# A Mamba block and a feed-forward block on one core: the group scale-and-shift, the end statistics, two bank places and one convolution tap change their place

## The chip, the cores and the metric

The kernel runs on one core of a Trainium2 chip. The metric is device time in microseconds (us), from the launch's first to its last instruction, the median of three runs. The engines of the core are TensorE (PE, matrix products; PEld is its weight load), VectorE (DVE), ScalarE (ACT), GpSimd (POOL) and SyncE (SP, which here only starts DMAs). Each has its own stream of instructions, runs it in the order in which it was written, and waits for the others on semaphores.

## The reference, cut to what matters

```python
# x is (8, 1024, 256) in float32: 8 batches, 1024 tokens, 256 channels
x = x + layernorm(attn(layernorm(x)))      # attn is a Mamba block
x = x + layernorm(ffn(layernorm(x)))       # ffn has weights of one sign bit and a scale

def attn(x):                               # 512 inner channels, 8 heads of 64
    xi, z = x @ Wx.T, x @ Wz.T
    xi = silu(causal_conv(xi, 4 taps) + conv_b)
    B, C = xi @ Wb.T, xi @ Wc.T
    dt = softplus(xi @ Wdt.T + b_dt)
    y = ssd_scan(xi, B, C, dt, -exp(log_a)) + d_param * xi
    y = (y - mean) / sqrt(var + eps) * gn_w + gn_b     # over all tokens and the 64 channels of a head
    return (y * silu(z)) @ Wout.T

def ffn(x):                                # 256 -> 1024 -> 256
    return gelu(x @ bw1.T + b1) @ bw2.T + b2
```

The group norm needs the whole sequence of a batch before its first output. So all that follows it (gate, output product, both residual sums, the feed-forward block) is a **tail** of the batch that can only begin when the batch's scan is through.

## The kernel before, in words

**Tiling.** A batch has 1024 tokens in two blocks j of 512 (BLK), and each block has four chunks q of 128 tokens. Channels lie on partitions, c counts the four groups of 128 inner channels (KI). `yT` holds the scan's output of a whole batch, `zs` the silu of the gate.

**Turns.** `turn_steps` writes one list of steps, a turn. In turn b the steps marked `own` belong to batch b, those marked `tail` to batch b-1, and a few at the end (`next`) to batch b+1. All five engines walk the same list (`all_batches`, `run`), and each carries out those steps for which it has a handler. So the list sets the order on each engine and nothing else does. There are eight turns; turn 0 has no tail steps, and after turn 7 comes `last_tail`. Turns 1 to 6 are alike.

**The steps that matter here**, with the lines of the profile:

- `xi` is the product with Wx (PE L1497) and two reads of its bank by ACT: the copy (L946) and the last tap with the bias (L953). `conv` is the other three taps on DVE (L1137); for (j, c) = (0, 0) they run in place in `hh`, lent for that time. Its two last arguments say which of the three taps are made. `silu` (ACT L981) and `xs_hi` (ACT L988) follow, `xs` (DVE L1142) makes the low half.
- `gn_sum` (DVE L1280 to L1285), `gn_mean` (PE L1652), `gn_root` (DVE L1289 to L1295, POOL L776) and `gn_fold` (DVE L1300 to L1304) turn the statistics of a batch into a scale and a shift for each channel. I call the application of the two to `yT` the **fold**: in the kernel before it is ACT's handler of the step `gate` (`head_normalise`, L1056), four instructions of 256 tokens for each (j, m). The other handlers of `gate` multiply by `zs`: DVE for j = 0 (L1311), POOL for j = 1 (L802). `Wo` is the output product (PE L1667 for j = 0), whose half m waits for the four gates of that half.
- `mid_stat`, `mid_norm`, `ff_stat`, `ff_norm` are the two layer norms around the residual sum. `ff_norm` writes `un` on ACT (L905). It waits for the root on POOL, which waits for the statistics on DVE. `uT` turns `un` on PE (L1507) and splits it on ACT (L1072) and DVE (L1339) into `uh`; `H` is the first feed-forward product (PE L1682), `O` the second (L1695).
- For each chunk: `ends` and `front` (PE L1598, L1579, L1587; `xdt` on DVE L1241; `Cd` and `xdw` on POOL L825 and L818), `score` (PE L1609, then `mt` on DVE L1250), `carry` (PE L1623 and L1632, the running `state` on POOL L836 and DVE L1256) and `back` (PE L1645, then `yT` on DVE L1266). The product L1623 of a chunk waits for its `xdw`, and the next chunk's L1632 for the new `state`.
- `end_stat` is the statistics of the last layer norm, on DVE (L1097 to L1107). It waits for POOL's bias sum (L788), the last part of `O`. `end_root` is on POOL (L766, L770), `end_norm` on ACT (L905, writes `y`), `end_add` on POOL (L793).

**Banks.** PSUM has eight banks. Five are the ring of the `own` steps: their products take the banks in turn, in the order of the list, and a product waits until the bank's last product has been read. A `None` in the list of keys skips one place, so that from there on the pairs (product, product before it in the same bank) are other ones. Two banks are the tail's, one is for the turned input and its like.

Of the kernel before, what the change touches and what calls it, by code (L numbers as in the profile page):

```python
# [20 lines left out]
NJ = T // BLK  # L21
NQ = BLK // P
# [116 lines left out]
def turn_steps(first, last):  # L139
# [16 lines left out]
    steps = []  # L156
    for j in range(NJ):
# [10 lines left out]
        elif j == 0:  # L168

            steps += own(("silu", 0, 0), ("xs_hi", 0, 0), ("xi", 0, 1), ("xi", 0, 2), ("xi", 0, 3))  # L170
            steps += tail(("head_stat", NJ - 1, 1), ("gn_sum",), ("gn_mean",)) + own(("conv", 0, 1, 0, 1)) + tail(("gn_root",))
            steps += own(("conv", 0, 1, 1, 3), ("z", 0, 0)) + tail(("gn_fold",)) + own(("conv", 0, 2, 0, 1), ("z", 0, 1))
            steps += tail(("gate", 0, 0)) + own(("xs", 0, 0), ("silu", 0, 1), ("xs_hi", 0, 1), ("conv", 0, 2, 1, 3))
            steps += own(("z", 0, 2), ("z", 0, 3)) + tail(("gate", 0, 1)) + own(("xs", 0, 1), ("conv", 0, 3))
            steps += tail(("Wo", 0, 0)) + own(*[("z_in", 0, c) for c in range(KI)])
# [16 lines left out]
        steps += own(("log", j))  # L192
        steps += tail(("mid_norm", j)) + own(("B", j, 1), ("decay", j)) + tail(("ff_stat", j), ("gelu_table",))
        if j == 0:
# [27 lines left out]
        steps += (norm if first else []) + own(("ends", j, 2), ("front", j, 2)) + (xT[0] if first else [])  # L222
        steps += own(("score", j, 2), ("carry", j, 1)) + xT[1] + own(("back", j, 1)) + tail(("end_stat", j), ("end_root", j))
        steps += own(("ends", j, 3), ("front", j, 3), ("score", j, 3))
        steps += [(who, "xi", nj, 0)] if j else []
        steps += own(("head_stat", 1, 0)) if j else []
        steps += own(("carry", j, 2)) + tail(("end_norm", j, 0), ("end_norm", j, 1)) + own(("back", j, 2))
        steps += tail(("gated", 1, 0)) if j == 0 else []
        steps += [(who, "conv", nj, 0)] if j else []
        steps += [(who, "silu_table")] + own(("carry", j, 3), ("back", j, 3))  # L230
# [13 lines left out]
def last_tail():  # L244

    def hidden(j, first, end):
        return [("H", j, f) for f in range(first, end)]

    steps = [("head_stat", NJ - 1, 1), ("gn_sum",), ("gn_mean",), ("gn_root",), ("gn_fold",)]
    steps += [("gate", j, m) for j in range(NJ) for m in range(2)]  # L250
    steps += [("Wo", 0, 0), ("Wo", 0, 1), ("mid_stat", 0), ("gated", 1, 0), ("gated", 1, 1), ("mid_norm", 0), ("ff_stat", 0), ("ff_norm", 0)]
    steps += [("Wo", 1, 0), ("Wo", 1, 1), ("mid_stat", 1), ("uT", 0), ("mid_norm", 1), *hidden(0, 0, 4)]
    steps += [("ff_stat", 1), *hidden(0, 4, 6), ("ff_norm", 1), *hidden(0, 6, 8), ("uT", 1), ("O", 0, 0), ("O", 0, 1)]
    steps += [*hidden(1, 0, 8), ("end_stat", 0), ("end_root", 0), ("end_norm", 0), ("end_add", 0)]
    steps += [("O", 1, 0), ("O", 1, 1), ("end_stat", 1), ("end_root", 1), ("end_norm", 1), ("end_add", 1)]
    return [("tail", *k) for k in steps]


def mamba_sandwich_kernel(nc, x, Wx, Wz, conv_w, conv_b, Wb, Wc, Wdt, b_dt, log_a, d_param, gn_w, gn_b,
                          Wout, w1, b1, w2, b2, out):  # L260
    ctx = ExitStack()
    with ctx:
# [158 lines left out]
        for who, kind, *at in turn_steps(False, False):  # L421
            if (who, kind, *at) == ("own", "carry", NJ - 1, NQ - 1):
                own_keys.append(None)
# [440 lines left out]
        def _(act):  # L864
# [209 lines left out]
            def hidden(t, j, f):  # L1074
# [8 lines left out]
                "log": step_log, "cums": cum_top, "skip": skip_term, "C": project_c, "decays": decay_exp, "front": front, "ends": ends,  # L1083
                "gate": head_normalise, "gated": gated_high, "uT": middle_high, "H": hidden})

# [641 lines left out]
```

## Time and profile before

| | |
|---|---|
| median of 3 runs | 1392.8 us (1391.0 to 1393.2) |
| the profiled execution | 1391.2 us, its span 1389.5 us |
| mean granted TensorE clock | 0.964 of full speed |
| busy: PE, DVE, ACT, POOL | 92%, 71%, 61%, 34% of the span |
| a turn, from 3.02 us PE wait to the same wait a turn later | 686.13 to 849.96, 163.8 us |

The span runs from the first to the last instruction. A view of waits gives, for an engine, how long it stood idle before instructions of a line and which instruction of another engine let it go on. A timeline lists instructions in order of time; in brackets stands the idle time before the first one and what ended it. In the table of windows, PEclk is the granted clock: 1.00 is 2.4 GHz, 0.50 is 1.2 GHz, and a value between them says that the stretch had both.

### The profile page before, as it was taken

The page shows a single profiled execution, that of the slowest core. Times are in us where ns is not written, and L with a number is a line of the kernel's source. Part 1 is how long each engine was busy: PE and PEld are TensorE (multiplying, and loading weights), DVE is VectorE, ACT ScalarE, POOL GpSimd, SP SyncE. Part 2 cuts the span into 40 slices and gives each one's busy share as a digit, 9 for nine tenths or more (in the row PEclk, how much of TensorE's full clock was granted, in tenths as well). Part 3 has the DMA queues.
Part 4 walks back from the last instruction along what each step waited for, and adds up shares of the span by engine and source line. Part 5 has one row for each costly group of instructions (what it writes and reads, how often), then busy time and mean ns, then how long its engine had stood idle before and what let it go on. Part 6 is the DMA issues. An engine that isn't in the chain of part 4 may idle for free.

```text
span 1389.5 us, 28357 instructions
## 1 busy us (share of the span) xinstructions
PE 1280.5 (92%) x10744; PEld 810.1 (58%) x10744; DVE 983.7 (71%) x2392; ACT 850.3 (61%) x1488; POOL 475.3 (34%) x575
## 2 busy tenths in 40 slices
PE   6999999999999999999999999999999999999765
PEld 3564647575565756656475664657556565756543
DVE  5674866868578676877758786686857777686574
ACT  5564675657755575665756676565666657565432
POOL 2031235133332533334342333514333253332533
PEclk9998999999999999999999999999999999999788
DMA  7010000101010010101001010010101000000100
GB/s 217 1 47 1 17 1 2 46 2 46 1 47 1 1 46 2 46 1 47 1 2 47 2 47 1 17 32 1 47 1 47 1 18 15 2 32 1 31 1 30
DMA packets 30566, 32.92 MB, mean 24 GB/s; under 512 B 1856, under 2 KB 28628, under 8 KB 30432
## 3 DMA queue, kind: packets, MB, share of 16 engines
q1 hardware_dynamic: 30432, 31.11, 7.0%
q8 instruction: 86, 1.41, 0.4%
q14 instruction: 48, 0.39, 0.1%
HBM read 22.72 MB, written 8.39 MB: 22 GB/s over the span
## 4 chain that ended last, share of the span: by engine, by line
PE 61%; DVE 19%; POOL 7%; issue 7%; ACT 6%; DVEq 0%; POOLq 0%; ACTq 0%
PE bank L1497 18%; PE bank L1682 8%; PE bank L1695 8%; PE bank L1667 4%; PE bank L1609 4%; PE bank L1663 3%; PE bank L1587 3%; ACT yT L1056 3%; PE bank L1645 2%; PE bank L1632 2%; PE bank L1579 2%; DVE un L1113 2%; DVE yT L1266 2%; PE bank L1623 1%; ACT un L905 1%
## 5 line engine op out<-in xcount | busy, mean ns | idle before, releaser
L1497 PE MATMUL bank<-sh,WbT 128*128 128x512 f16 x768 | 177.0, 387 | 6.7 <-DVE sh L1142 6.7
L1497 PE MATMUL bank<-sh,WcT 128*128 128x512 f16 x768 | 175.9, 379 | 0.0
L1682 PE MATMUL bank<-uh,sign1T 128*128 128x512 f16 x512 | 128.3, 398 | 23.1 <-DVE uh L1339 23.1
L1137 DVE SCALAR_TENSOR_TENSOR xs<-xi,vectors,xs 128x512 f32<-128x512 f32 x168 | 125.2, 749 | 11.6 <-ACT xs L953 8.2
L1497 PEld LDWEIGHTS bank<-sh,WbT 128*128 128x128 f16 x768 | 74.7, 99 | 95.3 <-issue 8.6
L825 POOL TENSOR_TENSOR Cd<-Cd,CT 128x512 f32<-128x512 f32 x64 | 81.5, 1273 | 137.0 <-ACT Cd L1048 137.0
L1497 PEld LDWEIGHTS bank<-sh,WcT 128*128 128x128 f16 x768 | 75.2, 98 | 86.9 <-issue 1.1
L1077 ACT ACTIVATE hf<-bank,vectors,alpha 128x512 f32<-128x512 f32 x128 | 99.1, 777 | 37.5 <-PE bank L1682 28.6
L1695 PE MATMUL bank<-sign2T,hh 128*128 128x256 f16 x1024 | 119.0, 275 | 1.8 <-DVE hh L1352 1.8
L1695 PEld LDWEIGHTS bank<-sign2T,hh 128*128 128x128 f16 x1024 | 100.9, 99 | 15.1 <-DVE hh L1352 2.6
L1250 DVE TENSOR_TENSOR mt<-bank,mt 128x512 f32<-128x512 f32 x128 | 82.3, 684 | 36.1 <-PE bank L1609 36.1
L1682 PEld LDWEIGHTS bank<-uh,sign1T 128*128 128x128 f16 x512 | 50.3, 102 | 87.9 <-DVE uh L1339 24.6
L1497 PE MATMUL bank<-xh,WxT 128*128 128x512 f16 x384 | 93.0, 395 | 2.2 <-DVE state L1256 2.2
L1048 ACT ACTIVATE Cd<-bank 128x512 f32<-128x512 f32 x64 | 38.1, 596 | 89.4 <-PE bank L1598 89.4
L1352 DVE SCALAR_TENSOR_TENSOR hh<-hf,hh 128x512 f16<-128x512 f32 x128 | 89.0, 696 | 4.4
L766 POOL TENSOR_TENSOR rstd_in<-var_eps_in,power 128x4 f32<-128x4 f32 x16 | 18.6, 1164 | 213.3 <-DVE var_eps_in L1107 213.3
L766 POOL TENSOR_TENSOR rstd_mid<-var_eps_mid,power 128x4 f32<-128x4 f32 x16 | 16.5, 1034 | 214.1 <-DVE var_eps_mid L1107 214.1
L905 ACT ACTIVATE un<-u,ln_shift_ff,rstd_ff 128x256 f32<-128x256 f32 x64 | 33.2, 589 | 88.0 <-POOL ln_shift_ff L770 88.0
L1497 PE MATMUL bank<-xh,WzT 128*128 128x512 f16 x384 | 85.6, 379 | 0.0
L1014 ACT ACTIVATE CT<-bank 128x512 f32<-128x512 f32 x64 | 37.7, 590 | 70.9 <-PE bank L1497 70.9
L1056 ACT ACTIVATE yT<-yT,gn_shift,gn_scale 128x256 f32<-128x256 f32 x128 | 65.1, 587 | 25.2 <-DVE gn_shift L1304 25.2
L1645 PE MATMUL bank<-mt,xdt 128*64 128x128 f32 x1024 | 77.1, 297 | 0.0
(212 smaller groups left out, 2757.2 us busy)
## 6 DMA issues: line engine op xcount, KB each, us to landing
xt<-L_attn_input_tensor_dram SPq DMA_DIRECT2D x16, 512.0 KB, 5.0
u<-L_attn_input_tensor_dram SPq DMA_DIRECT2D x16, 512.0 KB, 4.1
out_dram<-u SPq DMA_DIRECT2D x16, 512.0 KB, 2.9
yT<-in_L_ffn_w_dram SPq DMA_DIRECT2D x2, 512.0 KB, 9.9
u<-in_L_ffn_w_dram SPq DMA_DIRECT2D x2, 512.0 KB, 9.0
BT<-in_L_attn_Wx_dram SPq DMA_DIRECT2D x1, 512.0 KB, 4.8
BT<-in_L_attn_Wz_dram SPq DMA_DIRECT2D x1, 512.0 KB, 5.8
zs<-in_L_attn_Wb_dram SPq DMA_DIRECT2D x1, 512.0 KB, 5.5
```

Source lines behind the costliest of these rows:

```text
L825: pool.tensor_tensor(Cd[n % 2][:, :, :], Cd[n % 2][:, :, :], CT[:, :, q * P:(q + 1) * P], ALU.mult)\
L1056: nc.scalar.activation(v, v, ACT.Identity, bias=gn_shift[:, c:c + 1], scale=gn_scale[:, c:c + 1]).then_inc(yn_out.sem, 1)
L1077: nc.scalar.activation(hf[f % 2][:, :], bank(t, ("H", j, f))[:, :], ACT.Gelu, bias=b1_col[:, f:f + 1], scale=alpha1[:, f:f + 1]).then_inc( ...
L1137: nc.vector.scalar_tensor_tensor(out=conv_sum(j, c), in0=xi[:, c, k:k + BLK], scalar=taps[:, c, k:k + 1], in1=conv_sum(j, c), op0=ALU.mult ...
L1250: nc.vector.tensor_tensor(v, bank(t, ("S", j, q, g))[:, :], v, ALU.mult).then_inc(mt_out.sem, 1)
L1352: nc.vector.scalar_tensor_tensor(out=hh[1][:, f, :], in0=hf[f % 2][:, :], scalar=SG, in1=hh[0][:, f, :], op0=ALU.mult, op1=ALU.subtract).t ...
L1497: mm = nc.tensor.matmul(bank(t, key)[:, :], w[i][:, k, cols(m)], v[h][:, k, :], start=(a == 0), stop=(a == len(terms) - 1))
L1609: mm = nc.tensor.matmul(bank(t, key)[:, cols(c)], BT[rows, c, cols(q)], CT[rows, c, cols(q)], start=True, stop=True)
L1645: mm = nc.tensor.matmul(bank(t, key)[g * HD:(g + 1) * HD, cols(c // 2)], xdt[r][:, c * HP + g, :], mt[r][:, side(c * HP + g), c, :], start ...
L1667: mm = nc.tensor.matmul(bank(t, key)[:, (i % 2) * D:(i % 2 + 1) * D], yT[:, c, (j * NQ + i) * P:(j * NQ + i + 1) * P], WoutT[:, c, :], sta ...
L1682: mm = nc.tensor.matmul(bank(t, key)[:, :], sign1T[:, k, cols(f)], uh[i][:, k, :], start=(a == 0), stop=(a == len(terms) - 1))
L1695: mm = nc.tensor.matmul(bank(t, key)[:, (i % 2) * D:(i % 2 + 1) * D], hh[p][:, f, cols(i)], sign2T[:, f, :], start=(a == 0), stop=(a == le ...
```

## The change

1. ACT's fold gets a step of its own, `fold`. For the first half (j = 0) it stands right ahead of the same `gate` step as before. For the second half (j = 1), eight instructions, it goes from behind `ff_norm` and B's last product to a place ahead of `ff_stat` and `ff_norm`, behind the loading of the gelu table. The gates themselves stay.
2. `end_stat` goes ahead of `score` and `carry` of the chunk before (chunk 2 and 1), `end_root` behind `carry` 1.
3. A bank place is skipped ahead of the first `ends` of each block, and no longer ahead of the last `carry`.
4. In the next batch's first convolution group (0, 0) only two of DVE's three taps are made in the old turn. The third comes behind `gn_mean` in the new turn, and the taps of groups 1 and 2 are dealt out anew around `gn_root` and `gn_fold`. ACT's `silu` and `xs_hi` of group 0 go behind the three other `xi`.

```diff
-            steps += own(("silu", 0, 0), ("xs_hi", 0, 0), ("xi", 0, 1), ("xi", 0, 2), ("xi", 0, 3))
-            steps += tail(("head_stat", NJ - 1, 1), ("gn_sum",), ("gn_mean",)) + own(("conv", 0, 1, 0, 1)) + tail(("gn_root",))
-            steps += own(("conv", 0, 1, 1, 3), ("z", 0, 0)) + tail(("gn_fold",)) + own(("conv", 0, 2, 0, 1), ("z", 0, 1))
-            steps += tail(("gate", 0, 0)) + own(("xs", 0, 0), ("silu", 0, 1), ("xs_hi", 0, 1), ("conv", 0, 2, 1, 3))
-            steps += own(("z", 0, 2), ("z", 0, 3)) + tail(("gate", 0, 1)) + own(("xs", 0, 1), ("conv", 0, 3))
+            steps += own(("xi", 0, 1), ("xi", 0, 2), ("xi", 0, 3)) + tail(("head_stat", NJ - 1, 1), ("gn_sum",), ("gn_mean",))
+            steps += own(("conv", 0, 0, 2, 3), ("silu", 0, 0), ("xs_hi", 0, 0)) + tail(("gn_root",))
+            steps += own(("conv", 0, 1, 0, 2), ("z", 0, 0)) + tail(("gn_fold",)) + own(("conv", 0, 1, 2, 3), ("z", 0, 1))
+            steps += tail(("fold", 0, 0), ("gate", 0, 0)) + own(("xs", 0, 0), ("silu", 0, 1), ("xs_hi", 0, 1), ("conv", 0, 2))
+            steps += own(("z", 0, 2), ("z", 0, 3)) + tail(("fold", 0, 1), ("gate", 0, 1)) + own(("xs", 0, 1), ("conv", 0, 3))
...
-        steps += tail(("mid_norm", j)) + own(("B", j, 1), ("decay", j)) + tail(("ff_stat", j), ("gelu_table",))
+        steps += tail(("mid_norm", j)) + own(("B", j, 1), ("decay", j)) + tail(("gelu_table",))
+        steps += tail(*[("fold", 1, m) for m in range(2 if j == 0 else 0)], ("ff_stat", j))
...
-        steps += own(("score", j, 2), ("carry", j, 1)) + xT[1] + own(("back", j, 1)) + tail(("end_stat", j), ("end_root", j))
+        steps += tail(("end_stat", j)) + own(("score", j, 2), ("carry", j, 1)) + tail(("end_root", j)) + xT[1] + own(("back", j, 1))
...
-        steps += own(("carry", j, 2)) + tail(("end_norm", j, 0), ("end_norm", j, 1)) + own(("back", j, 2))
+        steps += tail(("end_norm", j, 0), ("end_norm", j, 1)) + own(("carry", j, 2), ("back", j, 2))
...
-        steps += [(who, "conv", nj, 0)] if j else []
+        steps += [(who, "conv", nj, 0, 0, 2)] if j else []
...
-            if (who, kind, *at) == ("own", "carry", NJ - 1, NQ - 1):
+            if kind == "ends" and at[1] == 0:
                 own_keys.append(None)
...
-                "gate": head_normalise, "gated": gated_high, "uT": middle_high, "H": hidden})
+                "fold": head_normalise, "gated": gated_high, "uT": middle_high, "H": hidden})
```

What this does to the streams is seen on two engines. PE and POOL have the same instructions in the same order as before (only the banks differ), and the last tail's order does not change on any engine.

On ACT, in turn 1 between the gelu table and the first C product's copy, the rows before were these (`CT` and `cum_hi` are the copies behind C(0, 0) and the running sums; `uh` is the split that `H` needs):

```order
L901 ACT_TABLE_LOAD
L901 ACTIVATE table_in<-ones 128x1
L905 ACTIVATE un<-u,ln_shift_ff,rstd_ff 128x256 x4
L1056 ACTIVATE yT<-yT,gn_shift,gn_scale 128x256 x8
L1014 ACTIVATE CT<-bank 128x512
L1021 ACTIVATE cum_hi<-bank 128x128
L1072 ACTIVATE uh<-bank 128x512 x2
```

and are now (the lines of the changed kernel are one higher from L194 on):

```order
L902 ACT_TABLE_LOAD
L902 ACTIVATE table_in<-ones 128x1
L1057 ACTIVATE yT<-yT,gn_shift,gn_scale 128x256 x8
L906 ACTIVATE un<-u,ln_shift_ff,rstd_ff 128x256 x4
L1015 ACTIVATE CT<-bank 128x512
L1022 ACTIVATE cum_hi<-bank 128x128
L1073 ACTIVATE uh<-bank 128x512 x2
```

The eight folds stood between the norm's output `un` and its split `uh`, and now stand ahead of both.

On DVE, in turn 1 at the end of block 0, from `xdt` of chunk 2 to `mt` of chunk 3, the rows before were

```order
L1241 TENSOR_TENSOR xdt<-bank,dt_t 128x512
L1250 TENSOR_TENSOR mt<-bank,mt 128x512 x2
L1256 TENSOR_TENSOR state<-state,bank 128x256
L1127 TENSOR_TENSOR xh<-bank,xh 128x512
L1266 TENSOR_TENSOR yT<-bank,yT 128x2x128 x2
L1097 BN_STATS stats_end<-y 128x6 x4
L1101 BN_AGGR moments_end<-stats_end 128x2 x4
L1106 TENSOR_SCALAR minus_mean_end<-moments_end 128x4
L1107 TENSOR_SCALAR var_eps_end<-moments_end 128x4
L1241 TENSOR_TENSOR xdt<-bank,dt_t 128x512
L1250 TENSOR_TENSOR mt<-bank,mt 128x512 x2
```

and are now

```order
L1242 TENSOR_TENSOR xdt<-bank,dt_t 128x512
L1098 BN_STATS stats_end<-y 128x6 x4
L1102 BN_AGGR moments_end<-stats_end 128x2 x4
L1107 TENSOR_SCALAR minus_mean_end<-moments_end 128x4
L1108 TENSOR_SCALAR var_eps_end<-moments_end 128x4
L1251 TENSOR_TENSOR mt<-bank,mt 128x512 x2
L1257 TENSOR_TENSOR state<-state,bank 128x256
L1128 TENSOR_TENSOR xh<-bank,xh 128x512
L1267 TENSOR_TENSOR yT<-bank,yT 128x2x128 x2
L1242 TENSOR_TENSOR xdt<-bank,dt_t 128x512
L1251 TENSOR_TENSOR mt<-bank,mt 128x512 x2
```

The ten instructions of the end statistics stood between `yT` of chunk 1 and `xdt` of chunk 3, and now stand ahead of `mt` of chunk 2, so that four groups (`mt`, `state`, `xh`, `yT`) come behind them.

On DVE, where turn 0 hands over to turn 1, the rows from `state` of the last chunk on are now as follows; before, all three taps of `hh` stood ahead of `state`, the first tap of group 1 stood where the third of `hh` stands now, and one tap of group 2 was made ahead of the first gates (L1312):

```order
L1138 SCALAR_TENSOR_TENSOR hh<-xi,vectors,hh 128x512 x2
L1257 TENSOR_TENSOR state<-state,bank 128x256
L1267 TENSOR_TENSOR yT<-bank,yT 128x2x128 x2
L1274 BN_STATS gn_stats<-yT 128x6 x4
L1281 BN_AGGR gn_mom<-gn_stats 128x2 x4
L1284 TENSOR_TENSOR gn_sq<-gn_mom 128x4
L1286 TENSOR_TENSOR gn_mom<-gn_mom,gn_sq 128x4
L1138 SCALAR_TENSOR_TENSOR hh<-xi,vectors,hh 128x512
L1290 COPY gn_head<-bank 128x8
```

So one tap fewer stands ahead of the group statistics, and between the two halves of the first gates there are now three taps in place of two.

## Rows read from the trace of the kernel before

**Rows 1.** The page, busy time, share of the span, number of instructions.

```profile
PE 1280.5 (92%) x10744; PEld 810.1 (58%) x10744; DVE 983.7 (71%) x2392; ACT 850.3 (61%) x1488; POOL 475.3 (34%) x575
```

**Rows 2.** Waits of PE, whole span: total us, times, longest us.

```profile
PE bank L1682 <- DVE uh L1339: 23.1, 8, 3.0
PE bank L1623 <- POOL xdw L818: 13.2, 14, 1.4
...
PE bank L1632 <- DVE yT L1266: 5.1, 8, 0.7
```

**Rows 3.** Timeline of ACT, turn 4, block 0: start, duration in us.

```profile
670.95 1.28 ACT L901 ACT_TABLE_LOAD   x1
672.24 0.20 ACT L901 ACTIVATE table_in<-ones 128x1 f32<-128x1 f32 x1
677.62 2.07 ACT L905 ACTIVATE un<-u,ln_shift_ff,rstd_ff 128x256 f32<-128x256 f32 x4 [5.18 <-POOL ln_shift_ff L770]
679.60 4.03 ACT L1056 ACTIVATE yT<-yT,gn_shift,gn_scale 128x256 f32<-128x256 f32 x8
```

**Rows 4.** Timeline of PE, first H products: turn 1 block 0, turn 4 blocks 0, 1.

```profile
195.68 1.90 PE L1682 MATMUL bank<-uh,sign1T 128*128 128x512 f16 x8 [3.02 <-DVE uh L1339]
...
686.13 3.22 PE L1682 MATMUL bank<-uh,sign1T 128*128 128x512 f16 x8 [3.02 <-DVE uh L1339]
...
766.61 1.89 PE L1682 MATMUL bank<-uh,sign1T 128*128 128x512 f16 x8
```

**Rows 5.** Windows: us; PE, PEld, DVE, ACT, POOL busy; PEclk; DMA share; GB/s.

```profile
160.00:1284.00 1124.00, 1072.60 (x9054) 676.75 (x9052) 824.02 (x2008) 721.24 (x1262) 397.11 (x460) 0.98 0.06 19
686.00:690.00 4.00, 3.87 (x12) 1.52 (x13) 3.71 (x9) 3.44 (x6) 0.00 (x0) 0.65 0.00 0
729.00:733.00 4.00, 3.59 (x40) 2.48 (x36) 3.42 (x9) 2.88 (x6) 2.36 (x3) 0.60 0.03 6
```

**Rows 6.** Timeline of PE, turn 4, end of block 0.

```profile
722.34 0.65 PE L1587 MATMUL bank<-ident,xs 128*128 128x128 f32 x4
...
725.37 0.67 PE L1632 MATMUL bank<-Cd,state 64*64 64x128 f32 x16 [0.23 <-DVE xdt L1241]
...
728.48 0.69 PE L1623 MATMUL bank<-xdw,bt 128*64 128x64 f32 x16 [1.42 <-POOL xdw L818]
729.58 0.97 PE L1632 MATMUL bank<-Cd,state 64*64 64x128 f32 x16 [0.41 <-DVE state L1256]
...
732.38 5.75 PE L1497 MATMUL bank<-xh,WxT 128*128 128x512 f16 x24
```

**Rows 7.** Timeline of DVE, turn 4, end of block 0.

```profile
717.31 0.69 DVE L1241 TENSOR_TENSOR xdt<-bank,dt_t 128x512 f32<-128x512 f32 x1 [0.57 <-PE bank L1587]
718.83 1.29 DVE L1250 TENSOR_TENSOR mt<-bank,mt 128x512 f32<-128x512 f32 x2 [0.83 <-PE bank L1609]
720.84 0.42 DVE L1256 TENSOR_TENSOR state<-state,bank 128x256 f32<-128x256 f32 x1 [0.72 <-POOL state L836]
...
721.87 0.75 DVE L1266 TENSOR_TENSOR yT<-bank,yT 128x256 f32<-128x256 f32 x2
722.53 1.39 DVE L1097 BATCH_NORM_STATS2 stats_end<-y 128x6 f32<-128x256 f32 x4
...
724.63 0.68 DVE L1241 TENSOR_TENSOR xdt<-bank,dt_t 128x512 f32<-128x512 f32 x1
```

**Rows 8.** Timeline of POOL, turn 4, the last bias sum of block 0.

```profile
715.74 1.27 POOL L788 TENSOR_TENSOR y<-y,b_row 128x512 f32<-128x512 f32 x1 [4.16 <-DVE y L1361]
```

**Rows 9.** Timeline of DVE, where turn 3 hands over to turn 4.

```profile
645.31 2.92 DVE L1137 SCALAR_TENSOR_TENSOR hh<-xi,vectors,hh 128x512 f32<-128x512 f32 x3
...
658.18 1.53 DVE L1137 SCALAR_TENSOR_TENSOR xs<-xi,vectors,xs 128x512 f32<-128x512 f32 x2
659.63 1.42 DVE L1311 TENSOR_TENSOR yT<-yT,zs 128x256 f32<-128x256 f32 x4
```

**Rows 10.** Timeline of PE, turn 4, the output product of block 0.

```profile
657.72 7.17 PE L1667 MATMUL bank<-WoutT,yT 128*128 128x256 f32 x32 [0.25 <-DVE yT L1311]
```

More of the change, by code:

```diff
@@ L249, in last_tail @@
     steps = [("head_stat", NJ - 1, 1), ("gn_sum",), ("gn_mean",), ("gn_root",), ("gn_fold",)]
-    steps += [("gate", j, m) for j in range(NJ) for m in range(2)]
+    steps += [(kind, j, m) for j in range(NJ) for m in range(2) for kind in ("fold", "gate")]
     steps += [("Wo", 0, 0), ("Wo", 0, 1), ("mid_stat", 0), ("gated", 1, 0), ("gated", 1, 1), ("mid_norm", 0), ("ff_stat", 0), ("ff_norm", 0)]
```

## The prediction

> **What bounds the kernel now.** I read the page first. PE is busy for 1280.5 us of the 1389.5 us span [rows 1], the others far less, so time can only come from two places: stretches in which PE stands still, and stretches in which it runs at half clock. The waits of PE [rows 2] say who holds it: the split `uh` (23.1 us in 8 waits, the longest 3.0), POOL's `xdw` (13.2 us in 14) and `yT` (5.1 us in 8). The timelines of turn 4 show where each stands, and the table of windows shows the clock around them.
>
> The 3.02 us wait is at the first H product of block 0 [rows 4]. Behind it PE is slow: the same eight products take 3.22 us there and 1.89 us in block 1, where there is no wait [rows 4]. The windows explain it: from 686 to 690 the granted clock was 0.65, that is 1.2 GHz for 2.8 of the 4 us, and from 729 to 733, behind the `xdw` wait, it was 0.60, 1.2 GHz for 3.2 us [rows 5]. Over turns 1 to 7 the mean is 0.98 [rows 5]: 0.02 of 1124 us, divided by the half that is missing, is some 45 us at 1.2 GHz. At about 3 us each these are some 14 stretches, two per turn. So a turn pays for these two stalls twice, first the stall, then the clock. Turn 1 is the exception: behind the same 3.02 us its eight products took 1.90 us, full speed [rows 4].
>
> **Part 1, the fold of the second half.** In the kernel before, ACT stands idle for 5.18 us until POOL's root comes, writes `un` from 677.62, then does eight folds, 4.03 us, and only then the copies that `uh` needs [rows 3]. The folds need only the group scale and shift, which are long there. Moved ahead of `un`, they can start when the gelu table's dummy is through, at 672.24 + 0.20 = 672.44, and end at 676.5, 1.1 us before `un` could start at 677.62. So ACT's idle time hides them. If they were later than that, `un` would be late by the difference. `uh` then comes 4.03 us sooner, PE's wait was 3.02, so the wait goes whole. It stands in turns 1 to 7: 7 x 3.02 = 21.1 us of the 23.1 in [rows 2] (the eighth wait, the other 2 us, is in the last tail). The clock loss behind it is 3.22 - 1.89 = 1.33 us; turn 1 had none [rows 4], so it counts in six, 8.0 us. Sum of part 1: **29 us**. POOL's gates of that half start sooner too, which nobody waits for.
>
> The margin of 1.1 us hangs on how soon ACT goes on behind the table load. The row shows the next instruction at 672.24, right at the end of the load at 670.95 + 1.28 = 672.23 [rows 3]. The Trainium skill, "ScalarE: Activation LUTs", section "What ACT_TABLE_LOAD costs", has a rule that speaks against this place: a switch costs a drain of about 1.38 us beside the load. By that rule the folds would end near 677.85 and `un` would be 0.2 us late in each of seven turns, a sum some 2 us smaller; this trace does not show the drain, and by it the sum is as above.
>
> **Part 2, the end statistics.** They hold DVE from 722.53 to the start of `xdt` at 724.63, 2.10 us [rows 7]. Behind that `xdt` of chunk 3 comes POOL's `xdw`, and behind that PE's L1623, which waits 1.42 us; with 0.23 for `xdt` and 0.41 for `state` around it PE loses 2.06 us at the end of block 0 [rows 6], and the clock stretch of 3.2 us costs half of itself, 1.6 us [rows 5]. Now the 2.10 us start behind `xdt` of chunk 2, at 718.0. Their input is there: the bias sum ends at 715.74 + 1.27 = 717.0 [rows 8]. They end at 720.1, and what is queued behind them slips: `mt` by 1.3 us, from 718.83 to 720.1. But `mt` was followed by 0.72 us of idle time, and `state` was ready at 720.84 [rows 7]: `state` starts at 721.3, 0.4 to 0.5 us late, and `yT` of chunk 1 as well. The turned `xs` of chunk 3 on PE (722.34, [rows 6]) waits for the bank that the first half of `yT` reads, which ended at 721.87 + 0.37 = 722.24. So it slips by 0.35 to 0.4 us. That is the price. For it, `xdt` of chunk 3 starts at 723.3 in place of 724.63 and `xdw` is ready about 725.1, when PE gets to L1623 only at 727.1. All three waits are gone and with them, I take it, the clock stretch: 2.06 + 1.6 - 0.4 = 3.3 us, in turns 1 to 7, **23 us**. Bounds: nothing gained, if the stall only moves to the place of the new one (then the 2.06 and the clock stay), and 3.7 if even the slip is hidden. The slip rests on rows 0.4 us apart, so I take the middle one.
>
> **Part 3, the hand-over of turns.** Of [rows 2], 13.2 - 8 x 1.42 = 1.8 us of `xdw` wait stand in the six ends of block 1 in turns 1 to 6, 0.3 each, and 0.7 each for `yT` [rows 2]. The first goes with part 2. The second is a wait for the bank of the last `carry`: through the skipped places its two `Y` products now follow products that `mt` and `state` read, which comes sooner than `yT`, so it goes too. The slip of 0.4 us stands against both. The group moments on DVE come sooner by this and by one tap of `hh`, 2.92 / 3 = 0.97 [rows 9]: together 0.97 + 0.3 + 0.7 - 0.4 = 1.6 us, and fold and gate with them. Of this something is given back. PE's first half of the output product takes 7.17 / 2 = 3.58 us [rows 10], and meanwhile DVE has one low half (0.6), two taps (1.53) and four gates (1.42), 3.55 us [rows 9]: just in time. With a third tap, 0.77 us, PE waits 0.7 us in the middle of the product. Net 1.6 - 0.7 = 0.9 us, in six turns, **5 us**. Where turn 0 hands over to turn 1 there are no end statistics, and the tap won and the tap lost cancel. Bounds: 0 and 1.6 each.
>
> **What costs nothing.** The skips ahead of `ends` pair the first products of a block with copies of C, which PE's next products wait for anyway. `silu` and `xs_hi` of group 0 go behind the three `xi` into 2 us in which ACT waited for the shift; their reader, B's first product, is more than 10 us off. The end of the last turn's block 1 has the 1.42 us wait as well, and a tail that hangs on DVE behind it: **1.6 us**, 2.0 less the slip.
>
> **Sum.** 29 + 23 + 5 + 1.6 = 59 us off the profiled execution's 1391.2 us, which gives 1332. That execution is 1.6 us under the median, so I forecast **1333 us** as a median, 4.3% faster.
>
> **The rivals.**
>
> *The clock does not come back.* The stalls go, but half-clock stretches turn up at other places, for instance around the new 0.7 us wait in the output product and the slip at the block's end. For it: turn 1 shows that the same stall can go with the loss or without it [rows 4], so where the clock falls is not fixed by the stall alone. Against it: the waits of 0.3 and 0.7 us stand at every hand-over today, and the count of two stretches per turn leaves none for them. Price: 8.0 + 7 x 1.6 = 19 us come back, 1352 us.
>
> *The stall only moves.* If the block of 2.10 us pushes `yT` and the bank behind it by more than the rows say, PE stalls at chunk 3's front and its clock falls there. Then parts 2 and 3 bring nothing, 59 - 30 = 29 us remain, 1363 us. For it: `yT`'s first half and the turned `xs` stand only 0.1 us apart today. Against it: 0.83 and 0.72 us of idle DVE time directly behind the new place.
>
> *Folds late, un late.* If anything holds ACT between the load and the end of the folds for more than the 1.1 us to spare, `un` is late. A pause as long as the load itself, 1.28 us, makes it 0.1 to 0.2 us in each of seven turns, 1333 for the profiled execution and 1334 as a median. The rule of the Trainium skill on table loads (section "What ACT_TABLE_LOAD costs") would be such a case; this trace speaks against it.
>
> *The end statistics hold the scan up.* This ends on the other side. `end_stat` now stands ahead of `mt` and `state`, and it waits for POOL's bias sum. If that came late by w, the whole scan would stand for w at 14 places. Today the sum is ready 1.0 us before DVE gets there, and PE has some 0.4 us more. To eat 59 us it must be 59 / 14 = 4.2 us late beyond that, a bias sum at 722.6 in place of 717.0. At 6 us of stall it would be 14 x 6 - 59 = 25 us slower, 1416. Nothing in the rows of POOL speaks for such a delay.
>
> *It does nothing*, because each gain is given back by the next wait of DVE, which is busy 71% of the span: 1391.
>
> **How the numbers follow.** My forecast 0.62; clock does not come back 0.12; stall moves 0.10; folds late 0.08; does nothing 0.04; slower 0.04. Two runs of this kernel differ by 0.15%, so 0.2% is about what tells from no change. The likeliest case has its own range by the bounds: 1332 less 7 x 0.4 and 6 x 0.7 at best, 1325; some 10 us more at worst, if half of part 2 and 3's clock and wait gains stay out, 1343. The range for 8 in 10 reaches over the clock rival up to where a moved stall would put it, 1324 to 1362; what is left out is half of the moved stall and the last two cases and a little below, some 0.15. Faster 0.92, same 0.04, slower 0.04.
>
> **What would show it.** Part 1: no wait of PE for `uh` over 0.2 us but in the last tail, eight folds ending before `un`, ACT's idle time before `un` near 1 us. Part 2: no wait for `xdw`; PE's turned `xs` of chunk 3 released by `yT`, 0.4 us. Part 3: a wait of L1668 for the gates in the middle of it, 0.7 us. Clock: a mean of 0.98 or more in place of 0.964. The forecast is wrong if the windows show 1.2 GHz anywhere in turns 1 to 7, or if a turn is longer than 157 us.

## The result, and the profile after

The changed kernel takes 1323.44 us, the median of 4 runs (1320.9 to 1327.82), against 1393.0 us for the kernel before beside it (1391.0 to 1394.17). The ratio is 0.9505 with an interval of 0.9473 to 0.9538: faster by 5%. The forecast was 1333 us with 1324 to 1362 for 8 in 10, so the median lies half a microsecond below the lower end.

The profiled execution took 1320.9 us, with a span of 1319.2 us. The page, as in [rows 1]:

```profile
PE 1255.9 (95%) x10744; PEld 798.6 (61%) x10744; DVE 985.7 (75%) x2392; ACT 852.6 (65%) x1488; POOL 480.9 (36%) x575
```

PE's busy time fell by 24.6 us with the same number of instructions: that is, in the main, clock. The span fell by 70.3 us; the other 45.7 are time in which PE stood idle. Windows of the kernel after: turns 1 to 7, the opening (all ahead of turn 1), the tail (all behind turn 7), with columns as in [rows 5]:

```profile
157.00:1237.00 1080.00, 1066.33 (x9278) 679.59 (x9278) 840.29 (x2042) 729.25 (x1273) 414.44 (x474) 1.00 0.06 19
...
0.00:157.00 157.00, 136.64 (x1176) 83.51 (x1176) 99.60 (x225) 89.04 (x159) 35.63 (x62) 0.98 0.21 62
1237.00:1319.20 82.20, 52.91 (x290) 35.48 (x290) 45.76 (x126) 34.35 (x57) 30.87 (x39) 0.82 0.08 26
```

The same cuts of the kernel before:

```profile
161.00:1305.00 1144.00, 1087.62 (x9278) 689.15 (x9278) 837.05 (x2044) 726.44 (x1272) 408.63 (x474) 0.98 0.06 18
...
0.00:161.00 161.00, 140.22 (x1176) 84.47 (x1176) 100.53 (x223) 89.50 (x160) 35.30 (x62) 0.96 0.20 61
1305.00:1389.50 84.50, 52.62 (x290) 36.44 (x290) 46.10 (x126) 34.34 (x57) 31.33 (x39) 0.78 0.08 25
```

In turns 1 to 7 PE stood still for 56 us before (1144.0 - 1087.6) and for 14 us after. The granted clock there went from 0.98 to 1.00. The cuts are at the first and the last group-mean product, L1653 (L1652 before). It comes once per turn, and from one to the next is the length of a turn: 163.8 to 164.1 us before in turns 2 to 6, 154.7 to 154.8 after. Turns 1 to 7 together became 63.6 us shorter. The other 6.7 us came in the opening and the tail, where the change does next to nothing: their clock was 0.98 and 0.82 in this execution, 0.96 and 0.78 before.

Waits of PE after (total, times, longest), to be held against [rows 2]:

```profile
PE bank L1668 <- DVE yT L1312: 9.8, 15, 4.9
...
PE bank L1653 <- DVE gn_mom L1286: 4.6, 8, 3.5
...
PE bank L1683 <- DVE uh L1340: 1.7, 1, 1.7
...
PE bank L1633 <- DVE state L1257: 0.4, 1, 0.4
```

The wait for `uh` is left once, in the last tail, and those for `xdw` and for `yT` (L1632 before, L1633 now) are gone. Seven short waits of L1668, the output product, are new.

**Part 1.** ACT in turn 4, block 0, as in [rows 3]:

```profile
640.96 1.28 ACT L902 ACT_TABLE_LOAD   x1
642.25 0.20 ACT L902 ACTIVATE table_in<-ones 128x1 f32<-128x1 f32 x1
642.36 4.03 ACT L1057 ACTIVATE yT<-yT,gn_shift,gn_scale 128x256 f32<-128x256 f32 x8
647.65 2.08 ACT L906 ACTIVATE un<-u,ln_shift_ff,rstd_ff 128x256 f32<-128x256 f32 x4 [1.27 <-POOL ln_shift_ff L771]
```

The folds begin directly behind the table's dummy and end 1.27 us before `un` can start: the 5.18 us of idle time have become 1.27. The dummy itself starts at 642.25, right at the end of the load (640.96 + 1.28 = 642.24). The Trainium skill, "ScalarE: Activation LUTs", section "What ACT_TABLE_LOAD costs", adds a drain of about 1.38 us there. By it the folds would have ended 0.1 us behind the time at which `un` could start (an estimate from that figure); this trace again shows no drain.

PE in the same turn: the output product, the first H product of block 0, and the end of block 0 (before: [rows 10, 4, 6]):

```profile
627.00 3.72 PE L1668 MATMUL bank<-WoutT,yT 128*128 128x256 f32 x16 [0.26 <-DVE yT L1312]
631.18 3.72 PE L1668 MATMUL bank<-WoutT,yT 128*128 128x256 f32 x16 [0.46 <-DVE yT L1312]
634.74 2.75 PE L1498 MATMUL bank<-sh,WbT 128*128 128x512 f16 x12
...
650.38 2.75 PE L1498 MATMUL bank<-sh,WcT 128*128 128x512 f16 x12
652.97 1.89 PE L1683 MATMUL bank<-uh,sign1T 128*128 128x512 f16 x8
654.70 2.75 PE L1498 MATMUL bank<-sh,WcT 128*128 128x512 f16 x12
...
688.12 0.66 PE L1588 MATMUL bank<-ident,xs 128*128 128x128 f32 x4
...
692.37 0.64 PE L1624 MATMUL bank<-xdw,bt 128*64 128x64 f32 x16
692.94 0.67 PE L1633 MATMUL bank<-Cd,state 64*64 64x128 f32 x16
693.53 1.09 PE L1646 MATMUL bank<-mt,xdt 128*64 128x128 f32 x16
694.56 5.35 PE L1498 MATMUL bank<-xh,WxT 128*128 128x512 f16 x24
```

No wait stands at H or at the end of block 0, and every duration there is that of full speed: 1.89 for 3.22, 0.67 for 0.97, 5.35 for 5.75.

**Part 2.** DVE in turn 4, as in [rows 7]:

```profile
682.82 0.69 DVE L1242 TENSOR_TENSOR xdt<-bank,dt_t 128x512 f32<-128x512 f32 x1 [0.56 <-PE bank L1588]
683.43 1.39 DVE L1098 BATCH_NORM_STATS2 stats_end<-y 128x6 f32<-128x256 f32 x4
...
685.53 1.28 DVE L1251 TENSOR_TENSOR mt<-bank,mt 128x512 f32<-128x512 f32 x2
686.72 0.41 DVE L1257 TENSOR_TENSOR state<-state,bank 128x256 f32<-128x256 f32 x1
687.05 0.68 DVE L1128 TENSOR_TENSOR xh<-bank,xh 128x512 f16<-128x512 f32 x1
687.65 0.74 DVE L1267 TENSOR_TENSOR yT<-bank,yT 128x256 f32<-128x256 f32 x2
```

The statistics hold `mt` up: it starts 2.71 us behind `xdt`, where it was 1.52 ([rows 7]), 1.2 us later. The idle time behind it takes most of that, and the rest reaches PE's turned `xs` through the bank that `yT` reads: it starts at 688.12, 0.72 us behind the start of L1580 (687.40), where it was 0.46 before (722.34 behind 721.88). The slip is 0.26 us.

### The profile page after: what moved, and what is told of

It reads as the page before. It is cut to its first block, busy times and chain, and to the rows that moved or that the text cites. A ratio compares the mean times of both kernels' runs of the same rounds, so it can differ in the third digit from the quotient of the medians.

```text
span 1319.2 us, 28349 instructions
## 1 busy us (share of the span) xinstructions
PE 1255.9 (95%) x10744; PEld 798.6 (61%) x10744; DVE 985.7 (75%) x2392; ACT 852.6 (65%) x1488; POOL 480.9 (36%) x575
## 4 chain that ended last, share of the span: by engine, by line
PE 48%; DVE 34%; issue 7%; ACT 6%; POOL 5%; DVEq 0%; POOLq 0%; ACTq 0%
PE bank L1498 13%; PE bank L1696 8%; PE bank L1683 8%; DVE xs L1138 7%; PE bank L1588 4%; PE bank L1610 4%; DVE sh L1143 2%; DVE yT L1267 2%; PE bank L1580 2%; DVE hh L1317 2%; ACT un L906 2%; PE bank L1508 2%; DVE gn_stats L1274 2%; DVE un L1114 2%; PE bank L1633 2%
## 5 line engine op out<-in xcount | busy, mean ns | idle before, releaser
L1498 PE MATMUL bank<-sh,WbT 128*128 128x512 f16 x768 | 173.2, 381 | 5.6 <-DVE sh L1143 5.6
L1498 PE MATMUL bank<-sh,WcT 128*128 128x512 f16 x768 | 175.9, 379 | 0.0
L1138 DVE SCALAR_TENSOR_TENSOR xs<-xi,vectors,xs 128x512 f32<-128x512 f32 x168 | 128.4, 768 | 5.8 <-ACT xs L954 2.1
L1498 PEld LDWEIGHTS bank<-sh,WbT 128*128 128x128 f16 x768 | 73.5, 98 | 91.6 <-DVE sh L1143 7.8
L1498 PEld LDWEIGHTS bank<-sh,WcT 128*128 128x128 f16 x768 | 75.2, 98 | 86.5
L1683 PE MATMUL bank<-uh,sign1T 128*128 128x512 f16 x512 | 121.8, 383 | 1.7 <-DVE uh L1340 1.7
L1498 PE MATMUL bank<-xh,WxT 128*128 128x512 f16 x384 | 87.4, 381 | 0.0
L1498 PE MATMUL bank<-xh,WzT 128*128 128x512 f16 x384 | 87.3, 384 | 0.0
L1610 PE MATMUL bank<-CT,BT 64*128 64x128 f32 x1024 | 74.4, 285 | 1.2 <-ACT mt L1039 1.2
L1362 DVE TENSOR_TENSOR y<-bank,alpha_row 128x512 f32<-128x512 f32 x30 | 20.8, 692 | 71.3 <-PE bank L1696 71.3
```

The source lines that it names most:

```text
L1138: nc.vector.scalar_tensor_tensor(out=conv_sum(j, c), in0=xi[:, c, k:k + BLK], scalar=taps[:, c, k:k + 1], in1=conv_sum(j, c), op0=ALU.mult ...
L1498: mm = nc.tensor.matmul(bank(t, key)[:, :], w[i][:, k, cols(m)], v[h][:, k, :], start=(a == 0), stop=(a == len(terms) - 1))
L1610: mm = nc.tensor.matmul(bank(t, key)[:, cols(c)], BT[rows, c, cols(q)], CT[rows, c, cols(q)], start=True, stop=True)
L1683: mm = nc.tensor.matmul(bank(t, key)[:, :], sign1T[:, k, cols(f)], uh[i][:, k, :], start=(a == 0), stop=(a == len(terms) - 1))
```

## The experiments

Twelve kernels, in three groups of four; a group ran on one chip, together with the kernel before. The medians of that were 1390.83, 1391.78 and 1391.62 us. "The turn" is again the distance of the group-mean products (L1653) of two turns, in the one profiled execution of each kernel. Where no clock fall comes or goes it differs by 0.2 us within a kernel, and the same turn of two executions of the kernel after agrees to 0.1 us. So it resolves more than a median of runs, in which the clock of opening and tail is mixed in.

**One part at a time, on the kernel before.** Fold alone: the steps `("fold", 1, m)` ahead of `ff_stat`. End statistics alone: the `end_stat` and `end_norm` lines of the diff. Banks alone:

```
-            if (who, kind, *at) == ("own", "carry", NJ - 1, NQ - 1):
+            if kind == "ends" and at[1] == 0:
```

Tap alone: the first block of lines of the diff, and where the next batch begins

```
-        steps += [(who, "conv", nj, 0)] if j else []
+        steps += [(who, "conv", nj, 0, 0, 2)] if j else []
```

In all four `fold` is a step of its own, and in the last three it stays at its old place, ahead of its gate.

> The kernel before with only the fold of the second half moved ahead of the feed-forward norm. Theory 'stall and clock are one debt': the 3.02 us wait for uh goes in seven turns and the clock loss of 1.3 to 1.7 us behind it in six, 29 to 31 us, so about 1363 us (ratio 0.978). PE waits for uh only in the last tail; the waits for xdw (13.2 us) and for yT (5.1 us) stay as they are. Rival 'the clock falls elsewhere': only the 21 us of waiting goes, 1372 us (0.985), and the mean granted clock stays at 0.964.

> The kernel before with only the end statistics moved ahead of the scores of chunk 2. Theory: the 1.42 us wait for xdw with 0.6 us around it goes in eight places and the clock loss behind it in seven, less a slip of 0.3 to 0.4 us at every block end, 23 to 26 us, so about 1368 us (0.982). The wait for xdw is gone, a wait of the turned xs for yT of 0.3 us comes up to 14 times, of which part may count as a short issue gap. Rival 'the stall only moves': 1391 to 1393 us, with the waiting booked on yT in chunk 3's front.

> The kernel before with only the two skipped bank places in place of the one. Theory 'banks hide behind DVE': the 0.7 us wait for yT shrinks to about 0.35 and the 0.36 us wait of the second xi goes, but the group moments on DVE come no sooner, so PE gives all of it back in front of them: 0 to 1 us, 1392 us (0.999 to 1.000). Rival 'the waits are additive': 0.7 us in six hand-overs, 4 us, 1389 us (0.997).

> The kernel before with only the third tap of group 0 and the taps behind it moved. Theory 'a tap won, a tap lost': the group moments come 0.97 us sooner, fold and first gates as well, and the output product then waits 0.6 us in its middle: net 0.3 us in seven hand-overs, 2 us, 1391 us (0.998 to 0.999). Rival: nothing is given back, 7 x 0.97 = 7 us, 1386 us (0.995).

| kernel | median us | ratio (95%) | turn us |
|---|---|---|---|
| fold alone | 1354.36 | 0.9751 (0.9715 to 0.9787) | 159.3, 158.1 in alternation |
| end statistics alone | 1360.61 | 0.979 (0.9754 to 0.9825) | 158.3 or 160.1 |
| banks alone | 1388.67 | 0.999 (0.9971 to 1.0009) | 161.2 to 164.2 |
| tap alone | 1388.35 | 0.9994 (0.9973 to 1.0016) | 163.8 |

The two large parts carry the result. Each is worth more alone than I had expected (36.5 and 30.2 us), and the sum of the two, 66.7, is more than both together bring (63, below). In turns 1 to 7 alone, without opening and tail, it is 34.3 and 30.5 us, and 61.3 together. The banks alone did as expected, nothing that is clear of the noise; their shortest turn, 161.2 us, is one in which neither stall was followed by a slow product. The tap alone was to bring 0.3 us a turn and brought none: the output product has its 0.46 us wait there as in the kernel after, and the turn stays at 163.8.

The windows of the kernel with the fold alone say why the two parts do not add up. These are the same place, the end of block 0 with its untouched wait for `xdw`, in turns 1, 2, 3 and 4:

```profile
233.00:237.00 4.00, 3.59 (x37) 2.35 (x35) 3.99 (x9) 2.81 (x6) 2.55 (x4) 0.60 0.01 4
391.00:395.00 4.00, 2.86 (x51) 2.19 (x52) 2.74 (x6) 3.97 (x8) 2.56 (x4) 1.00 0.00 0
551.00:555.00 4.00, 3.97 (x36) 2.65 (x37) 3.42 (x8) 2.35 (x5) 2.94 (x4) 0.57 0.00 0
710.00:714.00 4.00, 3.63 (x42) 2.26 (x43) 4.00 (x9) 3.12 (x7) 2.87 (x4) 1.00 0.02 6
```

And its PE in turns 2 and 3, each with the same wait:

```profile
391.73 0.69 PE L1624 MATMUL bank<-xdw,bt 128*64 128x64 f32 x16 [1.41 <-POOL xdw L819]
392.83 0.67 PE L1633 MATMUL bank<-Cd,state 64*64 64x128 f32 x16 [0.41 <-DVE state L1257]
...
549.93 0.69 PE L1624 MATMUL bank<-xdw,bt 128*64 128x64 f32 x16 [1.42 <-POOL xdw L819]
551.03 0.95 PE L1633 MATMUL bank<-Cd,state 64*64 64x128 f32 x16 [0.41 <-DVE state L1257]
```

One and the same wait was followed by a fall of the clock in every second turn. Taking out the fold's stall thus also spared three falls at the other stall, which either part would claim when taken alone. With the end statistics alone it was one: its first H product, behind the same 3.02 us wait, ran at full speed not only in turn 1 but in turn 5 too. A fall costs 1.25 us of the turn here (159.3 to 158.1) and 1.8 in the kernel with the end statistics alone.

**One part taken back, on the kernel after.** The same again, a run without the bank rule, one with the old hand-over, and one with neither (folds and end statistics only):

> The changed kernel once more, on the same chip as the three kernels of this call, so that they can be compared with it. 1321 to 1328 us as before, median 1323 to 1325. Two readings of the spread: if it is only the clock, the time follows the mean granted clock (each 0.001 of clock is 1319 x 0.001 / 2, near 0.7 us and in the tail less), and runs at 0.986 take 1321, runs at 0.979 take 1327.

> The changed kernel with the old bank place (one skip, ahead of the last carry). Theory 'banks do little alone, more together': with xdw in time, the second Y product of the last chunk would again wait for yT of the chunk before, and the third xi for the last state; 0.4 to 1 us in seven hand-overs, so 3 to 7 us slower than the changed kernel, 1327 to 1331 us. Rival 'hidden by DVE': the group moments set the hand-over anyway, 0 to 1 us, 1324 us.

> The changed kernel with the taps and silu of the old hand-over. Theory: the group moments come 0.97 us later, PE waits for them, fold and gates come later, but the output product is no longer held in its middle (0.46 us): net 0.5 us in seven hand-overs, 3.5 us slower than the changed kernel, 1327 us. Rival 'net nothing': 1324 us.

> The kernel before with the fold and the end statistics moved, the bank place and the taps as before. Theory 'these two are nearly all': turns of 155.2 us (0.03 for the bank and 0.4 for the taps over the changed kernel's 154.7), median near 1328 to 1330 us. Rival 'bank and taps only help together': each alone left out cost at most 0.4 us per turn, both left out cost 1 us and more, turns of 156 us and 1335 us.

| kernel | median us | ratio (95%) | turn us |
|---|---|---|---|
| after, again | 1327.42 | 0.9538 (0.9522 to 0.9554) | 154.74 |
| without banks | 1327.24 | 0.9534 (0.9516 to 0.9552) | 154.76 |
| without tap | 1326.9 | 0.9541 (0.9524 to 0.9559) | 155.14 |
| without both | 1328.72 | 0.9565 (0.9524 to 0.9606) | 155.14 |

The last of the four ran in another group, beside 1391.62 us; the others beside 1391.78. In the medians none of the four differs from the others. By the turns the tap is worth 0.40 us, near the 0.5 expected, and the banks 0.02, where I had expected 0.4 to 1: there the rival, "hidden by DVE", was right. The kernel without both came out as expected. Waits of the kernel without banks show where that term of mine went; the wait for `yT` is back, and the one for the group moments, eight times after, stands only in the last tail:

```profile
PE bank L1653 <- DVE gn_mom L1286: 3.5, 1, 3.5
PE bank L1633 <- DVE yT L1267: 2.1, 8, 0.7
```

The bank rule exchanges one wait on DVE for another on DVE: 0.15 us before the group mean in place of 0.20 at `Y`, the second product of `carry` (both read one by one in the timelines of PE; the 0.7 and the 3.5 above are at the end of the last turn).

The profiled execution of "after, again" had turns like the first one's and yet a span 7.2 us longer: 5.2 of it in the opening, which lasted 162.3 us at a granted clock of 0.94 where the first had 157.0 us at 0.98, and 1.6 in the tail, at 0.79 where the first had 0.82. Its median, 1327.42 us, lies above the 1323 to 1325 that I had expected.

**Is it PE's idle time that brings the clock down?** On the kernel before, 13 products with Wc that nobody reads were put ahead of the first H product of block 0. They fill 2.8 of the 3.02 us, and nothing comes sooner:

```
+                if j == f == 0 and ring_of(t, key) is not final:
+                    now, spare = t.ago(-1), ("C", 0, 2)
+                    pe.wait_ge(*empty(now, spare))
+                    for _ in range(13):
+                        nc.tensor.matmul(bank(now, spare)[:, :], WcT[0][:, 0, cols(2)], sh[0][:, 0, :], start=True, stop=True)
```

> The kernel before, with 13 matrix products of no use (128x512, into a free bank that C's third product overwrites) ahead of the first H product of block 0 in turns 1 to 7. They fill 2.8 us of the 3.02 us in which PE stands still, and wait for nothing; the fold stays behind the norm, so uh is as late as before. Theory 'stall and clock are one debt': the time of the stall stays, the clock fall behind it goes, 1.3 us in six turns; turns of 162.5 us in place of 163.8, and the whole 8 us faster, 1383 us. Rival 'the fall has nothing to do with the stall': turns stay at 163.8 us.

Measured 1377.43 us, 0.9907 (0.9877 to 0.9938). The place in turn 2 (the 13 products carry the name of `sh`):

```profile
350.20 2.97 PE L1682 MATMUL bank<-sh,WcT 128*128 128x512 f16 x13
353.39 1.90 PE L1687 MATMUL bank<-uh,sign1T 128*128 128x512 f16 x8 [0.22 <-DVE uh L1339]
```

The H product begins no sooner than before, but at full speed, 1.90 us for 3.35 in that turn of the kernel before. The idle time ahead is what the clock answered to, not the wait as such. The gain of 14 us is more than the 8 that I had expected of this one place: turns of 161.2 us, in which the end of block 0 shows no fall either, stand beside those of 162.7 with one, four to two in turns 1 to 6. So this kernel too was spared falls at the other stall, which it does not touch.

**What the slip and the taps cost.** `xT[1]`, the turning of the next batch's input, stands between the slipped `state` and `yT` of chunk 1. One kernel moves it behind `back`:

```
-    steps += tail(("end_stat", j)) + own(("score", j, 2), ("carry", j, 1)) + tail(("end_root", j)) + xT[1] + own(("back", j, 1))
+    steps += tail(("end_stat", j)) + own(("score", j, 2), ("carry", j, 1)) + tail(("end_root", j)) + own(("back", j, 1)) + xT[1]
```

A second does this and also moves one tap of `conv 0, 2` behind the second gates, `gate 0, 1`, which takes it out of the way of the output product:

```
-    steps += tail(("fold", 0, 0), ("gate", 0, 0)) + own(("xs", 0, 0), ("silu", 0, 1), ("xs_hi", 0, 1), ("conv", 0, 2))
-    steps += own(("z", 0, 2), ("z", 0, 3)) + tail(("fold", 0, 1), ("gate", 0, 1)) + own(("xs", 0, 1), ("conv", 0, 3))
+    steps += tail(("fold", 0, 0), ("gate", 0, 0)) + own(("xs", 0, 0), ("silu", 0, 1), ("xs_hi", 0, 1), ("conv", 0, 2, 0, 2))
+    steps += own(("z", 0, 2), ("z", 0, 3)) + tail(("fold", 0, 1), ("gate", 0, 1)) + own(("conv", 0, 2, 2, 3), ("xs", 0, 1), ("conv", 0, 3))
```

> The changed kernel with the second xT behind back 1 (one half of the kernel k). The slip of 0.3 us at both block ends should go: turns of 154.2 us in place of 154.7, 3 to 4 us faster than the changed kernel. If the gain of k came from the taps alone, turns stay at 154.7 us.

> The changed kernel with two more moves: the third tap of group 2 behind the second gates, and the second xT behind back 1, so that yT of chunk 1 comes ahead of the split of xh on DVE. Theory: the 0.46 us wait in the middle of the output product goes in seven turns (3 us) and the 0.3 us slip of the turned xs at 13 block ends (4 us), 7 us faster than the changed kernel, 1317 us. Rival: the split of xh, now later, is waited for by the next xi, or the low halves come too late for B, and nothing is won: 1323 to 1325 us.

The first took 1322.2 us, 0.9505 (0.9456 to 0.9555), turn 154.14; the second 1321.93 us, 0.9494 (0.9479 to 0.951), turn 153.95. So the slip cost 0.6 us a turn, 0.3 in each block, as expected. The tap's wait cost only 0.2, where I had counted 0.46, so that the second kernel fell short of its 1317 us. The PE timeline of it, turn 1, shows the output product in one piece again:

```profile
168.48 7.17 PE L1668 MATMUL bank<-WoutT,yT 128*128 128x256 f32 x32 [0.24 <-DVE yT L1312]
```

From its start to B it is 0.7 us shorter than in the first kernel, but from B to the first H product 0.5 us are lost again, at the turned `un`, which PE then reaches before ACT has written it. By its median this is the fastest version measured, 5.5 us under the kernel after that ran beside it (intervals of the ratios: up to 0.951 against from 0.9522).

**The statistics a chunk earlier still.** `end_stat` ahead of `ends` and `front` of chunk 2, so before its `xdt`. This was my try at the rival in which the statistics hold the scan up:

```
-    steps += (norm if first else []) + own(("ends", j, 2), ("front", j, 2)) + (xT[0] if first else [])
-    steps += tail(("end_stat", j)) + own(("score", j, 2), ("carry", j, 1)) + tail(("end_root", j)) + xT[1] + own(("back", j, 1))
+    steps += (norm if first else []) + tail(("end_stat", j)) + own(("ends", j, 2), ("front", j, 2)) + (xT[0] if first else [])
+    steps += own(("score", j, 2), ("carry", j, 1)) + tail(("end_root", j)) + xT[1] + own(("back", j, 1))
```

> The changed kernel with the end statistics one place further ahead, before front of chunk 2. DVE is there before the bias sum and waits 0.3 us for it, and xdt of chunk 2 comes 1.1 us later. Theory 'a wait of DVE counts only where PE reads its bank next': the second Y product of chunk 1 waits about 0.5 us for xdt, and the turned xs of chunk 3 no longer for yT; 0.1 to 0.4 us worse at each block end, turns of 155 to 155.5 us, 1328 to 1332 us. Rival 'the scan is held up': xdw of chunk 2 is late as well and PE stalls a microsecond or more, with the clock behind it: turns of 158 us and more.

Neither theory nor rival came true: 1322.91 us, 0.9524 (0.9484 to 0.9563), turns of 154.2 to 154.6, no slower than the kernel after. DVE of that kernel, turn 1:

```profile
220.96 1.46 DVE L1098 BATCH_NORM_STATS2 stats_end<-y 128x6 f32<-128x256 f32 x4
...
223.12 0.68 DVE L1242 TENSOR_TENSOR xdt<-bank,dt_t 128x512 f32<-128x512 f32 x1
223.72 1.28 DVE L1251 TENSOR_TENSOR mt<-bank,mt 128x512 f32<-128x512 f32 x2
225.60 0.42 DVE L1257 TENSOR_TENSOR state<-state,bank 128x256 f32<-128x256 f32 x1 [0.60 <-POOL state L837]
```

The bias sum on POOL runs from 220.35 to 221.63 here, and DVE starts the block at 220.96. It still does not wait: the first two of the four instructions read the half that was summed before, and the third starts at 221.66. So the sum comes just in time, with nothing to spare. `xdt` is late, but the chunk's products reach it late enough: PE waits for it once in the whole run, 0.2 us. What held of the expectation is that the turned `xs` of chunk 3 no longer waits for `yT`: in turn 1 it starts 0.51 us behind L1580, where the kernel after has 0.72, and that makes up for the rest. The rival, in which the statistics hold the scan up, is not borne out even one place further ahead.

## Why the prediction was right

Turn 4 on the two PE timelines, from start to start of the products named, closes the account:

| piece of turn 4 | before us | after us | gain |
|---|---|---|---|
| group mean to B, block 0 | 12.84 | 13.58 | -0.74 |
| B to first H, block 0 | 21.40 | 18.23 | 3.17 |
| first H to C behind it | 3.05 | 1.73 | 1.32 |
| C to `xi` (L1498) of block 1 | 43.20 | 39.86 | 3.34 |
| `xi` to `z` | 5.59 | 5.19 | 0.40 |
| `z` to B, block 1 | 10.42 | 10.42 | 0 |
| B to first H, block 1 | 18.22 | 18.49 | -0.27 |
| first H to the next group mean | 49.11 | 47.21 | 1.90 |

**Part 1** was forecast at 3.02 + 1.33 = 4.35 us a turn and measured 3.17 + 1.32 = 4.49. Each link held: load, folds, 1.27 us to spare (forecast 1.1), the wait gone whole, the H product at full speed, no loss in turn 1 to begin with.

**Part 2**: forecast 2.06 + 1.6 - 0.4 = 3.3, measured 3.34 + 0.40 = 3.74. The clock loss was 1.58: from the last L1633 to `xi` PE takes 692.94 to 694.56, 1.62 us, where it took 729.58 to 732.38, 2.80 ([rows 6]), 1.18 less, and `xi` 0.40 less. The slip was 0.26, not 0.4. The rest is a term that I had sized too small: the stretch from the turned `xs` to that L1633 shrank from 7.24 us ([rows 6]) to 4.82, so the three waits, 2.06 us in brackets, cost 2.42 (see the last section). 2.42 + 1.58 - 0.26 = 3.74.

**Part 3**: forecast 0.9, measured 1.90 - 0.74 - 0.27 = 0.89. The total is right; two steps of its working are not, and that the errors cancel is luck. The wait in the middle of the output product cost 0.7 us as forecast (0.74 in the table's first line, 0.46 of it shown as idle). But "it goes too" for the 0.7 us bank wait, as won by the skipped places, was wrong: without them the turn is as long. The end statistics are what shortens it. With them alone, and the banks as before, each of the six waits is 0.20 us where it was 0.70. The second step is block 1, of which my working had nothing but the slip of its end; -0.27 us stand there between B and the first H product. They are at the turned `un`, which ACT starts 12.90 us behind B's first product before (761.29 - 748.39) and 13.17 after (723.34 - 710.17):

```profile
761.29 2.07 ACT L905 ACTIVATE un<-u,ln_shift_ff,rstd_ff 128x256 f32<-128x256 f32 x4 [5.19 <-POOL ln_shift_ff L770]
...
723.34 2.08 ACT L906 ACTIVATE un<-u,ln_shift_ff,rstd_ff 128x256 f32<-128x256 f32 x4 [5.20 <-POOL ln_shift_ff L771]
```

At the head of its chain DVE starts the middle statistics (L1097, L1098 now) 0.62 us behind B before and 1.59 after. Why DVE comes there later was not followed.

**The sum** was 59 us in turns 1 to 7 and came to 63.6: 4.6 more, of which 7 x 0.15 = 1.0 are in part 1 and 7 x 0.44 = 3.1 in part 2; half a microsecond is not accounted for. The other 6.7 us by which the span shrank are not the change's but the clock of opening and tail: in "after, again" the two together lasted 245.6 us, in the first execution 238.8, and 245.5 in the kernel before. That execution's median lies inside the range, at 1327.42 us. So the first median fell just below the range because a term of part 2 was too small and because the clock outside the turns was by chance higher, both in one direction. The lower end, worked out from the bounds of my own terms, had no room for a spread that the runs of the kernel before do show from one execution to the next (1378.45 to 1393.46 in 23 runs on one chip).

**The rivals.** The clock did come back: 1.00 over turns 1 to 7, and the new 0.46 us wait was followed by no slow product. The sum counts a fall behind each stall from turn 2 on, as the kernel before had them (six behind the wait for `uh`, seven behind that for `xdw`). That is less firm than it looked: with one part alone, the stall that was left brought a fall in some turns only. With both stalls gone it did not matter. The stall did not move; its nearest form is the slip of 0.26 us. The folds were not late. The end statistics held nothing up, even one place earlier, where the bias sum has nothing left to spare. What I called the sign of an error, a turn of over 157 us or a clock under full in turns 1 to 7, did not appear.

## What to carry to other kernels

Price a stall of PE with the clock behind it: read the same product at a place with the stall and at one without, and count both. Then find the stall's own chain, and look on the engine that ends it for an instruction whose inputs have long been there and that could fill idle time ahead of the late one: eight folds and one block of statistics were worth 63 us, while the two edits that only shift which bank or which tap waits brought 0.4 us a turn together. A gain found with one edit alone is not to be added to another's when both spare the same clock falls.

## What the runs showed of the hardware

- The clock does not follow from a stall alone. The same 1.42 us wait with the 0.41 us one behind it was followed by a granted clock of 0.57 to 0.60 over 4 us in turns 1 and 3 and by 1.00 in turns 2 and 4 of one execution (fold alone). The 3.02 us wait was followed by H products at full speed, 1.90 us, in turns 1 and 5 and by slower ones, 2.61 to 3.47 us, in the other five (end statistics alone). Products that fill the idle time take the fall away: 1.90 us in all seven turns. What decides between the two cases stays open.
- A wait costs PE more than the idle time in brackets. From the start of the C product ahead to the start of the first H product it was 5.78 us before (680.35 to 686.13) and 2.59 after (650.38 to 652.97), 3.19 us for 3.02 of idle time. The C product's row is 2.75 us long, so in a running stream the profile's rows overlap by 0.16 us, and behind the wait they do not. At the end of block 0 it was 2.42 us for 2.06 in three waits.

```profile
680.35 2.75 PE L1497 MATMUL bank<-sh,WcT 128*128 128x512 f16 x12
```

- The span of the same kernel differs by 7 us between two executions with turns equal to 0.1 us. The opening, up to the first group mean, lasted 157.0 us at a mean clock of 0.98 and 162.3 us at 0.94.
